# Routed expert tiles: gate products from halves of the numbers, the queries' wait, gated values ahead of the outputs' scaling, and the tile loop written out

## What is computed

```
x = x + tanh(g_xattn[0]) * mlstm_cell(layernorm(x), ctx, ctx)          # layer 0
x = x + tanh(g_ffn[0])   * moe0(layernorm(x))     # 2 shared experts, 8 routed, the top 2 of each token
x = x + tanh(g_xattn[1]) * softmax_attention(layernorm(x), ctx)        # layer 1, 16 heads
x = x + tanh(g_ffn[1])   * moe1(layernorm(x))     # 1 shared, 16 small routed experts, top 4
expert(x) = (silu(x @ w1.T) * (x @ w3.T)) @ w2.T  # 256 -> 512 -> 256; "gate", "up", "down"
```

## Time and profile before

| | us |
|---|---|
| median of 3 runs | 909.86 |
| lowest and highest | 905.95, 913.98 |
| profiled execution, its own time | 906.93 |
| its span, first to last instruction | 905.1 |
| PE (TensorE matmul) busy | 794.4 |
| routed tiles: first gate product to last down product | 266.0 to 505.3 |

### The profile page before, as it was taken

How to read it: one execution, slowest core, us unless ns; L and a number is a source line. 1 busy time by engine, 2 the same in 40 slices (tenths; PEclk the granted TensorE clock), 3 DMA queues, 4 the chain that set the end, 5 groups by cost and what they waited for, 6 DMA issues and landing times.

```text
span 905.1 us, 15037 instructions
## 1 busy us (share of the span) xinstructions
PE 794.4 (88%) x5110; PEld 581.7 (64%) x5111; DVE 487.1 (54%) x1141; ACT 373.3 (41%) x759; POOL 218.1 (24%) x220
## 2 busy tenths in 40 slices
PE   4457399999999999999999867998778999999997
PEld 3345277788875555555555534565466888888886
DVE  4468865563342232223223477787775774765644
ACT  5468546232221111111111348877764425244222
POOL 0178110036411111111111375676320000000000
PEclk9788789999999999999999989999899999999999
DMA  9347650032421111111115540110103104050040
GB/s 303 121 191 281 247 209 7 1 111 83 147 76 41 47 41 46 41 47 41 42 46 143 167 150 11 40 47 17 56 1 75 21 1 118 1 118 1 19 100 23
DMA packets 33577, 74.13 MB, mean 82 GB/s; under 512 B 4400, under 2 KB 20400, under 8 KB 31888
## 3 DMA queue, kind: packets, MB, share of 16 engines
q1 hardware_dynamic: 30112, 64.03, 22.3%
q0 software_dynamic: 3408, 9.34, 2.9%
HBM read 61.73 MB, written 16.78 MB: 87 GB/s over the span
## 4 chain that ended last, share of the span: by engine, by line
PE 57%; DVE 13%; ACT 6%; issue 5%; DVEq 4%; DMA 1%; POOL 1%; POOLq 1%; SPq 0%; ACTq 0%
PE t_y_ps L2151 8%; PE t_up L2132 7%; PE t_gate L2132 4%; PE f_y L1739 4%; PE a_turned L976 3%; PE a_score L954 3%; PE a_score L956 3%; PE a_score L955 3%; PE t_h_turned L2140 3%; PE a_turned L880 2%; PE a_proj L853 2%; PE a_out_ps L976 2%; PE f_gate L1720 1%; PE f_gate L1721 1%; PE f_gate L1722 1%
## 5 line engine op out<-in xcount | busy, mean ns | idle before, releaser
L2186 ACT COPY t_hidT<-t_h_turned 128x512 f32<-128x512 f32 x39 | 22.9, 586 | 192.7 <-PE t_h_turned L2140 192.7
L2112 POOL DMA_INDIRECT outputs<-t_y,t_dest x39 | 37.4, 959 | 200.3 <-DVEq L2209 200.3
L2132 PE MATMUL t_gate<-W,t_xT 128*128 x156 | 73.7, 595 | 1.2 <-DVE t_xT L2194 1.2
L2151 PE MATMUL t_y_ps<-W,t_hidT 128*128 x312 | 73.9, 380 | 0.8 <-ACT t_hidT L2186 0.8
L2132 PE MATMUL t_up<-W,t_xT 128*128 x156 | 73.4, 593 | 0.0
L2194 DVE COPY t_xT<-t_x_turned 128x256 f32<-128x256 f32 x39 | 16.6, 425 | 98.0 <-PE t_x_turned L2122 98.0
L1142 ACT CAST a_hhi<-a_hid 128x512 fp32r<-128x512 f32 x48 | 29.8, 620 | 82.2 <-DVEq L1436 81.4
L2151 PEld LDWEIGHTS t_y_ps<-W,t_hidT 128*128 128x128 f32 x312 | 56.3, 190 | 7.5 <-issue 1.5
L1438 DVE TENSOR_TENSOR a_hlo<-a_hid,a_hhi 128x512 fp32r<-128x512 f32 x48 | 33.2, 692 | 35.2 <-ACT a_hhi L1142 35.2
L1131 ACT ACTIVATE a_act_g<-a_score 128x512 f32<-128x512 f32 x48 | 28.7, 597 | 51.6 <-PE a_score L956 51.4
L2208 DVE TENSOR_SCALAR t_y<-t_y_ps,t_dest 128x256 f32<-128x256 f32 x39 | 18.9, 484 | 53.0 <-PE t_y_ps L2151 53.0
(11 more groups left out here) (389 smaller groups left out, 2048.3 us busy)
## 6 DMA issues: line engine op xcount, KB each, us to landing
W<-in_w_dram SPq DMA_DIRECT2D x9, 1536.0 KB, 8.4
a_cb<-comb_rows SPq DMA_DIRECT2D x16, 512.0 KB, 7.9
W<-m_rows SPq DMA_DIRECT2D x14, 512.0 KB, 4.8
slot_tokens<-in_blank_rows_dram SPq DMA_DIRECT2D x1, 5031.0 KB, 22.4
t_x<-slot_tokens SPq DMA_DIRECT2D x39, 129.0 KB, 2.0
a_raw<-in_w_dram SPq DMA_DIRECT2D x3, 1536.0 KB, 7.1
a_picked<-outputs SPq DMA_DIRECT2D x8, 512.0 KB, 8.4
X<-in_x_dram SPq DMA_DIRECT2D x4, 512.0 KB, 6.2
```

What stands on the lines that cost most here:

```text
L2112: pool.indirect_dma_start(y_dram, bass.IndirectOffsetOnAxis(ap=dest[p][:, 0:1].bitcast(U32), axis=0), y[p][:], None).then_inc(y_stored[p], 16)
L2132: last = pe.matmul(out[p][:], xT[p][:, k], W[:, ds(e, 1), at:at + HID], start=(k == 0), stop=(k == KT - 1))
L2151: last = pe.matmul(y_ps[p][:, 0:D], hidT[p][:, h], W[:, ds(e, 1), at:at + D], start=(h == 0), stop=(h == HT - 1))
```

## The change

1. Gate products of the routed tiles are made from halves: six `F32R` products in place of two `F32` ones. The tokens' `xT_hi` is made by ScalarE (`keep_xhi`), `xT_lo` by VectorE in `keep_x`; the plain `xT` stays, for up.
2. The routed experts' gate weights are split in the shared stage, one expert in each of eight units (`SPLIT`): ScalarE rounds 128x1024, VectorE subtracts in place. Experts 0 and 1 are split in units 29 and 30. So that this fits, the silu's output and the hidden values share buffers, `LATE_COLS` grows from 1536 to 2560, the tokens' halves are stored as `x_halves`, and layer 1's buffers are placed in another order.
3. TensorE's body becomes gates(i+1), turn_x(i+2), turn_hidden(i), ups(i+1), down(i).
4. VectorE computes hid(i+1) (`middle(i, p)`, the instruction that made hid(i) in the body before) ahead of the scaling of y(i).
5. `over` writes all 39 bodies out, on all engines.
6. `(0, "x", 1)` is moved ahead of `(1, "v", n)` in `by_dve`.

```diff
+        SPLIT = {16: 3, 17: 4, 18: 5, 25: 6, 26: 7, 28: 2, 29: 0, 30: 1}
+            def split_hi(u):
+                e = SPLIT[u]
+                act.wait_ge(w_loaded[e], 16)
...
+                act.copy(W_hi[:, e], W[:, e, 0:KT * HID]).then_inc(whi_ready, 1)
+            def split_lo(u):
+                e = SPLIT[u]
+                dve.wait_ge(whi_ready, nth_split[e])
+                gates = W[:, e, 0:KT * HID]
+                dve.tensor_tensor(gates.bitcast(F32R), gates, W_hi[:, e].bitcast(F32), ALU.subtract).then_inc(wlo_ready, 1)
...
         def over(eng, body):
-            body(0, 0, 1)
-            body(1, 1, 2 - 1)
-            pairs = (NT - 5) // 2
-            with eng.Fori(0, pairs) as j:
-                body(j * 2 + 2, 0, j + 2)
-                body(j * 2 + 3, 1, j + 2)
-            for i in range(2 + 2 * pairs, NT):
+            for i in range(NT):
                 body(i, i % 2, i // 2 + 1)
...
+            def gates(i, p, e):
+                pe.wait_ge(xT_ready, i + 1)
                 wait(pe, hid_ready, i - 1)
                 for k in range(KT):
+                    cols = slice(k * HID, (k + 1) * HID)
+                    pe.matmul(gate[p][:], xT_hi[p][:, k], W_hi[:, ds(e, 1), cols], start=(k == 0), stop=False)
+                    pe.matmul(gate[p][:], xT_hi[p][:, k], W[:, ds(e, 1), cols].bitcast(F32R), start=False, stop=False)
+                    last = pe.matmul(gate[p][:], xT_lo[p][:, k], W_hi[:, ds(e, 1), cols], start=False, stop=(k == KT - 1))
+                last.then_inc(gate_ready, 1)
...
                 e = expert(i)
                 if inside(i, NT - 1):
                     e_next = expert(i + 1)
-                    product(i + 1, 1 - p, gate, 0, gate_ready, e_next)
+                    gates(i + 1, 1 - p, e_next)
+                if inside(i, NT - 2):
+                    turn_x(i + 2, p, nth + 1)
                 turn_hidden(i, p)
                 if inside(i, NT - 1):
-                    product(i + 1, 1 - p, up, 1, up_ready, e_next)
-                if inside(i, NT - 2):
-                    turn_x(i + 2, p, nth + 1)
+                    ups(i + 1, 1 - p, e_next)
                 down(i, p, e)
...
                 act.activation(act_g[p][:], gate[p][:], ACT.Silu).then_inc(silu_ready, 1)
+                if inside(i, NT - 2):
+                    keep_xhi(i + 2, p)
...
             def keep_x(i, p):
-                dve.wait_ge(xt_ready, i + 1)
+                dve.wait_ge(xhi_ready, i + 1)
                 wait(dve, up_ready, i - 1)
-                dve.tensor_copy(xT[p][:].rearrange("p k t -> p (k t)"), x_turned[:, 0:D]).then_inc(xT_ready, 1)
+                dve.tensor_copy(xT[p][:].rearrange("p k t -> p (k t)"), x_turned[:, 0:D])
+                dve.tensor_tensor(xT_lo[p][:].rearrange("p k t -> p (k t)"), x_turned[:, 0:D],
+                                  xT_hi[p][:].rearrange("p k t -> p (k t)").bitcast(F32), ALU.subtract).then_inc(xT_ready, 1)
                 dve.tensor_copy(next_dest[p][:], x[p][:, D:D + 2].bitcast(I32)).then_inc(dest_ready, 1)
...
             def body(i, p, nth):
                 wait(dve, y_stored[p], (nth - 1) * 16)
                 dve.tensor_copy(dest[p][:], next_dest[p][:])
                 dve.drain()
                 if inside(i, NT - 2):
                     keep_x(i + 2, p)
+                if inside(i, NT - 1):
+                    middle(i + 1, 1 - p)
                 dve.wait_ge(down_ready, i + 1)
...
-        by_dve = [(0, "v", 0), (0, "v", 1), (1, "v", 0), (1, "v", 1), (0, "x", 1)]
+        by_dve = [(0, "v", 0), (0, "v", 1), (0, "x", 1), (1, "v", 0), (1, "v", 1)]
```

More of the change, by code:

```diff
@@ L570, in attention_tiles @@
             sb(n, [128, 512], F32R)
-        for n in ("act_g0", "act_g1", "hid0", "hid1"):
+        for n in ("act_g0", "act_g1"):
             sb(n, [128, 512])
         sb("raw1", [128, WN])
+        sb("block2hi", [128, WN], F32R)
+        sb("block2lo", [128, WN], F32R)
+        sb("between", [128, 2048 + 4 * 512 + 512])
         sb("xn", [128, CH, D])
@@ L1716, in gate_up @@
                 whi, wlo = shared[b]
-                tokens = slice(c * 512, (c + 1) * 512)
+                xhi, xlo = (x_halves[:, c, half] for half in range(2))
                 for dst, cols in ((gate, gate_cols), (up, up_cols)):
                     for k in range(KT):
-                        pe.matmul(dst[q][:], whi[:, cols(k, ht)], xhi[:, k, tokens], start=(k == 0), stop=False)
-                        pe.matmul(dst[q][:], whi[:, cols(k, ht)], xlo[:, k, tokens], start=False, stop=False)
-                        last = pe.matmul(dst[q][:], wlo[:, cols(k, ht)], xhi[:, k, tokens], start=False, stop=(k == KT - 1))
+                        pe.matmul(dst[q][:], whi[:, cols(k, ht)], xhi[:, k], start=(k == 0), stop=False)
+                        pe.matmul(dst[q][:], whi[:, cols(k, ht)], xlo[:, k], start=False, stop=False)
+                        last = pe.matmul(dst[q][:], wlo[:, cols(k, ht)], xhi[:, k], start=False, stop=(k == KT - 1))
                 last.then_inc(gu_ready, 1)
@@ L2124, in turn_x, with ups @@
                 last.then_inc(xt_ready, 1)
-            def product(i, p, out, part, ready, e):
-                if part == 0:
-                    pe.wait_ge(xT_ready, i + 1)
+            def gates(i, p, e):
+                pe.wait_ge(xT_ready, i + 1)
                 wait(pe, hid_ready, i - 1)
                 for k in range(KT):
-                    at = (part * KT + k) * HID
-                    last = pe.matmul(out[p][:], xT[p][:, k], W[:, ds(e, 1), at:at + HID],
-                                     start=(k == 0), stop=(k == KT - 1))
-                last.then_inc(ready, 1)
+                    cols = slice(k * HID, (k + 1) * HID)
[3 more added lines that the diff above has]
+                last.then_inc(gate_ready, 1)
+            def ups(i, p, e):
+                wait(pe, hid_ready, i - 1)
+                for k in range(KT):
+                    at = (KT + k) * HID
+                    last = pe.matmul(up[p][:], xT[p][:, k], W[:, ds(e, 1), at:at + HID], start=(k == 0), stop=(k == KT - 1))
+                last.then_inc(up_ready, 1)
             def turn_hidden(i, p):
@@ L2170, in _ @@
             pe.wait_ge(choice_done, 1)
-            pe.wait_ge(w_loaded, 16 * (E0 + 1))
+            pe.wait_ge(late_loaded, 16)
+            pe.wait_ge(wlo_ready, E0)
             e0 = expert(0)
-            product(0, 0, gate, 0, gate_ready, e0)
-            product(0, 0, up, 1, up_ready, e0)
+            gates(0, 0, e0)
             turn_x(1, 1, 1)
+            ups(0, 0, e0)
             over(pe, body)
@@ L2214, in _ @@
             dve.drain()
+            middle(0, 0)
             over(dve, body)
@@ L2283, in _ @@
             def _(pool):
[L2285 removed]
+                pool.wait_ge(before[4], NSH0 * HT * NCH)
                 for p in range(2):
```

106 lines of the change are left out of this document (63 added, 43 removed).

## The result

The changed kernel takes 885.02 us, the median of four runs from 882.22 to 890.36, against 910.99 (905.95 to 913.98) for the kernel before on the same chip: a ratio of 0.9727, with a 95% interval of 0.9662 to 0.9793. The forecast was 886.6, in a range from 878 to 898.

The account below looks back on a forecast made before the run. TensorE's stream was taken to bound the tiles. Tiles -21.0, closing part -2.0 and start -0.3 gave -23.3 us, other terms 0; against the median of 909.86 that made 886.6, range 878 to 898.

Parts of the forecast that it names:

- What bounds: Routed tiles: bound by TensorE's stream; a loop body costs 6.08 us, of which 0.25 isn't TensorE's work.
- Gate from halves: Gates of the tiles: 1.72 us removed, six rounded products at 0.23, 1.38, added; -0.34 a tile.
- bound at 0.216: Gate products in the tiles: the low end of the range takes the product at 0.216, -3 us.
- rival (a): Gate products: register operation not hidden behind short products, 0.276 each; +11 us, 898; chance 0.10.
- The new order: TensorE's body: 5.49 us if nothing waits, with hidT's cover 0.7 us and other engines' additions costing nothing.
- The loop's gap: Loop body: 0.25 us that isn't TensorE's work goes by moving `middle` alone; writing out adds nothing more.
- Sum over the tiles: Gate of tile 1 to last down's end: 37 bodies at 5.49, -21.0 us; the closing part -2.0.
- The start: First tiles: gates(0) 0.7 us later, gates(1) at about 270.2 in place of 270.50; -0.3, between -0.6 and +0.9.
- Code loading: Written-out loop: one round becomes 17, 7 loads more, perhaps 10; cost put at nothing.
- rival (c): Written-out tiles: code loading makes the kernel slower than before, 922 us at 3.5 us a load; chance 0.04.
- Splitting and the queries' wait: Shared stage: gate-weight splits cost 0, up to +2 us; layer 1: queries 1.6 earlier, gain 0, at best -1.6.
- Rival (d): Layer 1: new placing and phase shift TensorE's lower clock level; 2 to 4 us either way, no separate chance.

Follow-up runs that it names:

- the fixed addresses: Changed kernel with four of the six gate products of every tile reading expert 0's high halves at a fixed address: 883.92 us, one run, beside 908.06.

## Why the prediction was right, point by point

**What bounds.** Right. With TensorE's stream as the bound of the tiles, the sum of its pieces gave the body: 5.49 forecast, 5.493 measured.

**Gate from halves.** Right in size: six products at 0.23. Forecast -0.34 a tile, or 12.9 us over the 38 gates of the stretch; taken away alone, 12.1. The sign named for it, 1.38 from the gates' first start to turn_x's, came out as 1.59 by the way the border is recorded; the whole body holds it. The bound at 0.216 wasn't reached, and neither was the one of 0.276: rival (a) falls with the fixed addresses, which gave nothing. It had also counted two register operations too many. TensorE is busy 211.32 of the 212.10 us from gates(1) to the end of the last down, over 99%.

**The new order.** The covers held. hidT's cover was put at 0.7 and is 0.93. The sentence behind it, that each further 0.1 us would cost 4 us, has the right sign and the wrong place: 0.87 us more of ScalarE's work cost 9.8, and cost it at the gates.

**The loop's gap.** Here the working was wrong though its sum was right. "So the gap of 0.25 goes, by the move of `middle` alone" holds for a body with plain gates (222.63). So does the opposite, that writing out alone takes it (224.45). And for the body as changed neither is enough. "The branch goes on all engines; its share of the 0.25 us is in the sum above already" looked at VectorE's branch; TensorE's own comes due when the gates get short, 3.60 us. Both edits were in the change, so the sum didn't notice.

**Sum over the tiles.** 37 bodies: 472.90 - 269.62 = 203.28, forecast 203.13. From the gate of tile 38 to the end of the last down 481.72 - 472.90 = 8.82, forecast 8.69. Together -22.7 against -23.0.

**The start.** Gates(0) waits 1.34 in place of 0.60: 0.74 later, forecast 0.7. From the turning of tile 0 to gates(1) it is 4.94 instead of 5.50; -0.56, forecast -0.3. The other 0.32 of the -0.88 had come before the tiles began. VectorE's small copy, which was to hold it until 268.79, takes 0.56 us after the change (266.18 to 266.74), and gates(1) waits for nothing: TensorE's own stream sets its start.

**Code loading.** The loads went from 35 to 44 in the largest queue and from 22 to 27 in the next. That is 14 more, where 7 to 10 were forecast for both together. But no body is longer than 5.50, so rival (c) falls.

**Splitting and the queries' wait.** Both at nothing, and within the bounds given: the doubled rounding shows the room (1.3 us lost at the stage's end for another 1.05 a split), and the old order costs 0 to 0.9 in a chain that the total doesn't show. Open is the idle time of ScalarE behind the second split, 4.95 us and more, on the two chips on which the kernel before has no trace; the working looked for nothing there.

**The sum and the clock.** -23.3 forecast to the end of the last down, -23.55 measured. Against the profiled spans only -16.9 is left, since this execution spent 41.7 us of layer 1 at the lower clock and the one before 21.1; the medians of four runs each differ by 25.97. Rival (d) was right that a few us of layer 1 come and go, though the same kernel shows it from run to run and no new placing is needed. It sized them at 2 to 4 either way; the four runs lie 8 apart, and the profiled pair differs by 6.65. That the median came within 2 us of the forecast was luck in that term.

## What to carry to other kernels

Where one engine's stream fills a loop, the new body is the sum of its start-to-start intervals, and here it could be added up to 0.01 us from rows of the old trace. But ask of every engine's sequencer, the bound one's above all, what it must do between two instructions (value loads, 942 ns a body here; the loop's branch, 215 ns; a wait passed 0.18 us ahead of its product in place of 0.90), because making products shorter takes away its time and not only other engines'. Edits that each hide the same gap must be undone one by one, in both kernels, before a gain is put down to one of them. And before the profiled spans of two kernels are compared, the granted clock over each stage is.

## What the runs showed of the hardware

- In the loop of the kernel before TensorE's branch takes 215 ns in the median and up to 243 (shown above; 215 and 244 with the loop back). From the same view, of the other engines:

```profile
L2086 ACTq COMPARE_BRANCH  x17: 40/45/45, 290.8 to 485.2; - x17
...
L2086 DVEq COMPARE_BRANCH  x17: 50/56/63, 295.1 to 489.5; - x17
...
L2086 POOLq COMPARE_BRANCH  x17: 40/45/50, 295.6 to 490.0; - x17
```

- In the changed kernel (L2184) one expert number, read from `tile_expert` into TensorE's registers, takes 302 ns in the median and up to 497, and its register operation another 151; with the 18 of the third operation, two numbers take 942 ns of down's 1.73 us.
- With the tokens' rounding three times, TensorE's sequencer goes on to down 0.18 us ahead of down's first product instead of 0.90. No product of down shows a wait for t_hidT but the last tile's (0.8, as in the changed kernel). The first weight loads of the gates (L2153; in the body shown at 346.43, 1.9 us behind down's first product) have idle time in front of them 39 times, 16.8 us in all, where the changed kernel has 2 times and 2.0, and the tiles are longer by 0.26 us a body.
- In the changed kernel the first of GpSimd's drains among its additions took 4.54 us, the other five 2.53 to 2.60 (L789). With one brought forward, which itself took 8.35 us beside a wait for data (L781), the six among the additions took 1.35 to 2.65. What a drain waits for there wasn't tried.
- An execution spent 21 us of layer 1 at the lower clock, 0.50 (the kernel before), and another 44 (the same with VectorE's order changed in the tiles), with the same instructions there.
